# One-core layer kernel: query and key weights packed on chip, mask products in four row groups, padded one-hot and spreading matrices, new step orders

## The reference, cut to what matters

```
qm = split(q @ Wq.T + bq); km = split(k @ Wk.T + bk); vm = split(v @ Wv.T + bv)
scores = einsum(qm, km) / 4
scores = where(mask, scores, -1e8)
out = (softmax(scores) @ vm) @ Wo.T + bo
```

```
weights = one_hot(top1(logits)) * softmax(logits)
y = (gelu(x @ W_cols + b_cols) * weights).reshape(...) @ proj_w + proj_b + x
```

## Time and profile before

| what | value |
|---|---|
| median of three runs | 2304.79 us (2304.69 to 2305.6) |
| the profiled execution's own time | 2305.36 us |
| its span, first to last instruction | 2303.6 us |
| mean granted TensorE clock | 0.974 of full speed |
| PE, PEld, DVE, ACT, POOL busy | 92%, 78%, 72%, 60%, 34% |
| DMA | 30.12 MB, 33,954 packets, nearly all in the first 45 us |

### The profile page before, as it was taken

How to read it: one execution, slowest core, us unless ns; L and a number is a source line. 1 busy time by engine, 2 the same in 40 slices (tenths; PEclk the granted TensorE clock), 3 DMA queues, 4 the chain that set the end, 5 groups by cost and what they waited for, 6 DMA issues and landing times.

```text
span 2303.6 us, 81126 instructions
## 1 busy us (share of the span) xinstructions
PE 2130.6 (92%) x33068; PEld 1805.7 (78%) x33130; DVE 1657.9 (72%) x5290; ACT 1374.1 (60%) x4262; POOL 778.8 (34%) x1835
## 2 busy tenths in 40 slices
PE   4799999999999999999999999999999999999976
PEld 3687888888878777878888888878878878788864
DVE  3478777777777677777777877767877777777743
ACT  3465556766555765556776555666555666555642
POOL 2233243333233333233343324333324333224321
PEclk8799999999999999999999999999999999999997
DMA  6000000000000000000000000000000000000000
GB/s 208 7 8 10 10 10 7 5 9 10 10 10 7 4 9 10 10 10 7 5 9 9 10 10 7 4 9 10 10 10 7 4 9 9 9 10 7 7 4 5
DMA packets 33954, 30.12 MB, mean 13 GB/s; under 512 B 17680, under 2 KB 31008, under 8 KB 32816
## 3 DMA queue, kind: packets, MB, share of 16 engines
q1 hardware_dynamic: 33584, 24.94, 3.6%
...
## 4 chain that ended last, share of the span: by engine, by line
PE 77%; DVE 14%; ACT 4%; issue 3%; SPq 2%; POOL 1%; DVEq 0%; DMA 0%; POOLq 0%
PE bank_b L641 11%; PE bank_a L463 10%; PE bank_b L738 5%; PE bank_a L473 4%; PE bank_b L761 4%; PE bank_b L649 4%; PE bank_b L602 4%; DVE y1p L1142 3%; PE bank_a L579 3%; PE bank_a L535 3%; PE bank_a L511 3%; PE bank_b L692 3%; ACT prob L926 2%; PE bank_a L586 2%; PE bank_a L545 2%
## 5 line engine op out<-in xcount | busy, mean ns | idle before, releaser
L1013 DVE SCALAR_TENSOR_TENSOR acc<-ypad,convw,acc 128x128 f32<-128x128 f32 x1536 | 429.0, 343 | 112.4 <-ACT acc L815 112.1
L463 PE MATMUL bank_a<-xnT,wqkvz 128*128 128x128 f32 x2048 | 250.6, 279 | 2.0 <-DVE u L1089 2.0
L463 PEld LDWEIGHTS bank_a<-xnT,wqkvz 128*128 128x128 f32 x2048 | 241.4, 194 | 6.2 <-DVE u L1089 4.3
L926 ACT ACTIVATE prob<-bank_b,nmax 128x128 f32<-128x128 f32 x512 | 182.2, 381 | 39.4 <-DVE nmax L1163 38.6
L1378 POOL TENSOR_TENSOR ostat<-ostat 128x4 f32<-128x4 f32 x64 | 20.4, 320 | 504.3 <-ACT gseg L880 502.2
L1424 POOL TENSOR_SCALAR lnv<-mv 128x1 f32<-128x1 f32 x128 | 26.1, 204 | 362.5 <-DVE mv L1103 357.2
L815 ACT ACTIVATE acc<-bank_a,convw 128x128 f32<-128x128 f32 x512 | 148.0, 395 | 0.0
L535 PE MATMUL bank_a<-zblk,kkT 32*32 32x32 f32 x8192 | 119.5, 195 | 22.3 <-DVE zblk L1073 15.6
L906 ACT ACTIVATE prob<-bank_b 128x512 f32<-128x512 f32 x64 | 38.2, 597 | 167.4 <-PE bank_b L641 167.4
L535 PEld LDWEIGHTS bank_a<-zblk,kkT 32*32 32x32 f32 x8192 | 93.7, 107 | 55.8 <-issue 44.5
L545 PE MATMUL bank_a<-ablk,xblk 32*32 32x32 f32 x8192 | 120.0, 195 | 18.6 <-DMA bk<-in_bk_dram 15.1
...
## 6 DMA issues: line engine op xcount, KB each, us to landing
xin<-in_x_dram SPq DMA_DIRECT2D x32, 128.0 KB, 2.0
cin<-in_ctx_dram SPq DMA_DIRECT2D x32, 128.0 KB, 2.1
out_dram<-yout SPq DMA_DIRECT2D x32, 128.0 KB, 1.7
...
```

The lines of the kernel that those rows point to most:

```text
L463: last = mm(A[bank][:, b * P:(b + 1) * P], wqkvz[:, c, o:o + P], xnT[:, c, :], start=(c == 0), stop=(c == KC - 1))
L926: last = fn(prob[:, j, b, :], Bk[j][:, b * P:(b + 1) * P], ACT.Exp, scale=HD ** -0.5, bias=nmax[:, 4 * j + b:4 * j + b + 1], accum_out=esu ...
L1013: stt(acc[:, c, :], ypad[:, c, k:k + P], convw[:, c, k:k + 1], acc[:, c, :], ALU.mult, ALU.add).then_inc(conv.sem, 1)
```

## The change

1. `Wq` and `Wk` are loaded whole (512 KB each, zeros included) into the space of `probT` (named `raw`), two DMAs in place of 16; at the start of trip 2, after the wait for `w_b`, POOL copies the used columns in eight operations to `wq` and `wk`. `b_k` and `b_q` wait for it (`packed`) for the first element.
2. The mask product of bank `j` has 32 rows: a matrix whose rows 0, 32, 64 and 96 are one and whose others are zero (`row0_bf`) against rows 32j to 32j + 31 of `fill_bf`, in row group `j`.
3. `onehot` is 128 x 128 (columns 16 to 127 stay zero) and `wT` and `spread_bf` have 128 rows (rows 16 to 127 of `spread_bf` stay zero), so that the transpose, the copy and the spreading products use 128 rows and columns.
4. All four orders are new. The trips are cut at another point (greatest lag 2, so 34 trips), and steps have other neighbours.

```
+            ("iota", NCOL), ("parity", 2), ("row0", 1)):
+    put("row0", (p % 32 == 0) * 1.0)
 ORDER = dict(
-    pe="b_v@2 b_x2T@2 a_lb01@1 a_la10@1 b_router@2 b_gu0@2 b_gu1@2 a_la11@1 a_lb10@1 b_gu2@2 a_la20@1 "
-       "a_lb11@1 b_gu3@2 b_dn0@2 a_lb20@1 a_la21@1 b_dn1@2 a_lb21@1 a_vT0@1 a_la30@1 b_k@2 a_la31@1 a_lb30@1 "
-       "a_lb31@1 b_y1T@2 a_pa@1 b_q@2 a_pb@1 c_s a_mt@1 c_pT0 a_vT1@1 a_xT a_sz0@1 c_pT1 a_ba a_qkv0 c_pT2 "
-       "a_o0@1 a_sz1@1 c_pT3 a_qkv1 a_o1@1 c_pv c_R a_z0 a_z1 c_xo a_qkv2 a_qkv3 c_y2T a_dec0 c_h a_ss c_lg "
-       "c_c0 a_st c_c1 c_wT a_kk c_spread a_dec1 c_pj0 b_oT0 b_oT1 c_pj1 b_w0 b_w1 a_la00 b_cT a_qk a_la01 "
-       "a_lb00".split(),
-    act="b_sum@2 b_cT@2 b_x2T@2 b_sg0@2 b_rl@2 b_sg1@2 b_rt@2 a_mix2@1 a_mix3@1 a_sum b_y1T@2 a_zf@1 b_q@2 "
-       "a_zo@1 c_exp0 a_mt@1 c_exp1 a_xT c_exp2 a_sz0@1 c_exp3 a_ba a_qkv0 a_o0@1 a_sz1@1 c_pT0 c_pT1 a_qkv1 "
-       "a_o1@1 c_R a_ln a_z0 a_mix0 a_z1 a_seg a_mix1 a_sq c_y2T c_h a_qkv2 a_st c_lt a_qkv3 c_c0 c_te c_wT "
-       "c_c1 a_dec0 a_dec1 b_oT0 b_oT1".split(),
-    dve="a_lb31@1 a_pa@1 b_k@2 a_u0@1 c_y4@3 c_max0 c_max1 a_xn c_max2 a_low@1 a_u1@1 c_max3 c_pT0 a_conv00 "
-       "a_conv01 c_pT1 a_conv02 c_rec a_core0@1 a_conv10 c_ao a_conv11 a_core1@1 c_sum2 a_conv12 c_y2 c_lb "
-       "c_route a_conv20 a_ss c_gc0 c_weight c_gc1 a_lower a_init c_sum3 b_hid a_la00 c_y3 b_x2 a_la01 "
-       "a_lb00 a_conv21 b_v a_conv22 a_lb01 a_conv30 a_la10 a_conv31 a_la11 a_lb10 b_act0 b_top a_conv32 "
-       "a_la20 a_lb11 a_score b_act1 b_ys0 a_la21 a_lb20 b_ys1 a_lb21 a_la30 a_la31 b_y1 a_lb30".split(),
-    pool="c_y2b@3 a_rq@1 c_ln2@3 b_xh@2 b_rs@2 b_rd@2 b_rt@2 c_ln3@3 a_xr@1 b_ln0@2 b_y1b@2 a_x a_osc0@1 a_ga "
-       "a_osc1@1 a_g c_ln1 c_rx b_mask c_sig a_sc".split(),
+    pe="a_la11@1 b_gu3@2 a_lb11@1 a_la20@1 b_dn0@2 a_la21@1 a_lb20@1 b_dn1@2 a_lb21@1 a_la30@1 a_vT0@1 b_k@2 "
+       "a_la31@1 a_lb30@1 a_lb31@1 b_y1T@2 a_pa@1 b_q@2 a_pb@1 c_s a_mt@1 a_vT1@1 a_xT c_pT0 a_sz0@1 c_pT1 "
+       "a_ba a_qkv0 c_pT2 a_o0@1 a_sz1@1 c_pT3 a_qkv1 a_o1@1 c_pv c_R a_z0 a_z1 c_xo a_qkv2 a_qkv3 a_ss "
+       "c_y2T a_dec0 c_h a_st c_lg c_c0 c_c1 c_wT a_dec1 c_spread a_kk c_pj0 b_oT0 b_oT1 c_pj1 b_w0 b_w1 "
+       "a_la00 b_cT a_la01 a_lb00 b_v a_qk b_x2T a_lb01 a_la10 b_router b_gu0 b_gu1 b_gu2 a_lb10".split(),
+    act="b_sg1@2 b_rt@2 a_sum a_mix2@1 a_mix3@1 b_y1T@2 a_zf@1 b_q@2 a_zo@1 c_exp0 a_mt@1 c_exp1 a_xT c_exp2 "
+       "a_ba a_sz0@1 c_exp3 a_qkv0 a_o0@1 a_sz1@1 c_pT0 c_pT1 a_qkv1 a_o1@1 c_R a_ln a_mix0 a_z0 a_z1 a_mix1 "
+       "a_sq a_qkv2 a_st c_y2T c_h a_qkv3 c_lt a_seg c_c0 c_wT c_c1 c_te a_dec0 a_dec1 b_oT0 b_oT1 b_cT "
+       "b_sum b_x2T b_rl b_sg0".split(),
+    dve="a_lb10@1 b_act1@2 a_la20@1 a_lb11@1 b_ys0@2 a_la21@1 a_lb20@1 b_ys1@2 a_lb21@1 a_la30@1 a_la31@1 "
+       "b_y1@2 a_lb30@1 a_lb31@1 a_pa@1 b_k@2 a_u0@1 a_xn c_max0 c_max1 c_max2 a_low@1 a_u1@1 c_max3 c_pT0 "
+       "a_conv00 c_pT1 c_rec a_conv01 a_conv02 a_conv10 a_conv11 c_ao a_core0@1 a_core1@1 a_conv12 c_sum2 "
+       "c_y2 a_conv20 a_conv21 a_conv22 c_lb a_ss c_route c_gc0 c_weight c_gc1 a_lower a_init c_sum3 b_hid "
+       "a_la00 c_y3 b_x2 a_la01 a_lb00 a_conv30 a_conv31 b_v a_lb01 a_score a_la10 c_y4 b_top b_act0 "
+       "a_conv32 a_la11".split(),
+    pool="b_xh@2 a_rq@1 b_rd@2 a_xr@1 b_rt@2 b_ln0@2 a_x b_y1b@2 b_mask a_osc0@1 a_ga a_osc1@1 a_g c_ln1 c_y2b "
+       "c_rx c_sig a_sc c_ln2 b_rs c_ln3".split(),
 )
-        spread_bf = sb("spread_bf", [NCOL, 8 * P], BF16)
+        spread_bf = sb("spread_bf", [P, 8 * P], BF16)
+        row0_bf = sb("row0_bf", [P, P], BF16)
-        onehot = sb("onehot", [P, NCOL])
-        wT = sb("wT", [NCOL, P], BF16)
+        onehot = sb("onehot", [P, P])
+        wT = sb("wT", [P, P], BF16)
-        dense_qk = [(w[:, :, P * o:P * o + P].rearrange("p k (j c d) -> p k j c d", j=4, c=2)[:, i, :, c, :],
-                     w_d.rearrange("p k (a j t) -> p k a j t", a=4, j=4, t=32)[:, i, 2 * o + c, :, 0:HD])
-                    for w, w_d in ((wq, wq_d), (wk, wk_d)) for i in range(KC) for o in range(2) for c in range(2)]
+        raw = probT[:, :, :, :].rearrange("p a b f -> p (a b f)").rearrange("p (w k f) -> p w k f", w=2, k=KC)
+        raw_qk = [(raw[:, i, :, :], w_d) for i, w_d in enumerate((wq_d, wk_d))]
...
             def c_s(n):
-                    mm(quad(Bk[j]), ident_bf[:, :], fill_bf[:, :].unsqueeze(1).to_broadcast([P, 4, P]), start=True, stop=False)
+                    r = slice(32 * j, 32 * j + 32)
+                    mm(quad(Bk[j]), row0_bf[r, :], fill_bf[r, :].unsqueeze(1).to_broadcast([32, 4, P]), start=True, stop=False)
...
             def c_wT(n):
-                tr(Bk[0][0:NCOL, 0:P], onehot[:, :], ident).then_inc(wT_ps.sem, 1)
+                tr(Bk[0][:, 0:P], onehot[:, :], ident).then_inc(wT_ps.sem, 1)
...
-                fn(wT[:, :], Bk[0][0:NCOL, 0:P], ACT.Copy).then_inc(wT_ok.sem, 1)
+                fn(wT[:, :], Bk[0][:, 0:P], ACT.Copy).then_inc(wT_ok.sem, 1)
...
+            nc.vector.tensor_copy(row0_bf[:, :], con("row0").to_broadcast([P, P])).then_inc(prep.sem, 1)
+            nc.gpsimd.memset(spread_bf[:, :], 0.0).then_inc(filled.sem, 1)
+            nc.gpsimd.memset(onehot[:, :], 0.0).then_inc(filled.sem, 1)
...
             def before_b():
                 pool.wait_ge(w_b.sem, W_B)
+                for i, w in enumerate((wq, wk)):
+                    for o in range(2):
+                        for c in range(2):
+                            dense = w[:, :, P * o:P * o + P].rearrange("p k (j c d) -> p k j c d", j=4, c=2)[:, :, :, c, :]
+                            padded = raw[:, i, :, P * (2 * o + c):P * (2 * o + c) + P].rearrange("p k (j t) -> p k j t", j=4)[:, :, :, 0:HD]
+                            ts(dense, padded, 1.0, 0.0, ALU.mult, ALU.add).then_inc(packed.sem, 1)
```

More of the change, by code:

```diff
@@ L55 @@
                       ("level1", BLK), ("levels", len(LEVELS) * BLK), ("eye_blocks", BLK),
-                      ("iota", NCOL), ("parity", 2)):
+                      ("iota", NCOL), ("parity", 2), ("row0", 1)):
     CONST[_name] = (_at, _at + _width)
@@ L306, in build @@
         w_a, w_b = sig("weights_a"), sig("weights_b")
+        packed = sig("packed", 8)
         wqkvz_in = [sig(f"wqkvz_in{g}") for g in range(6)]
@@ L369, in build @@
         W_A = 16 * (len(loads_a) + len(small_a))
-        W_B = 16 * (len(loads_b) + len(small_b) + len(dense_wo) + len(dense_qk) + len(dense_b))
-        FILLS = 5
-        PREP = 7
+        W_B = 16 * (len(loads_b) + len(small_b) + len(dense_wo) + len(raw_qk) + len(dense_b))
+        FILLS = 7
+        PREP = 8
         def heads(t, half):
@@ L420, in _ @@
                 sp.dma_start(dst[:], src).then_inc(w_b.sem, 16)
-            for dst, src in small_b + dense_wo + dense_qk:
+            for dst, src in small_b + dense_wo + raw_qk:
                 sp.dma_start(dst, src).then_inc(w_b.sem, 16)
@@ L653, in b_k @@
                 pe.wait_ge(*ysum(n, 2))
+                if first(n):
+                    pe.wait_ge(*packed(1))
                 for b in range(2):
@@ L1210, in c_route @@
                 dve.wait_ge(*lchain(n, 4))
-                ts(onehot[:, :], con("iota"), lsm[:, 0:1], None, ALU.is_equal).then_inc(lchain.sem, 1)
+                ts(onehot[:, 0:NCOL], con("iota"), lsm[:, 0:1], None, ALU.is_equal).then_inc(lchain.sem, 1)
                 ts(lsm[:, 1:2], lmax[:, 0:1], -0.5, None, ALU.mult).then_inc(lchain.sem, 1)
@@ L1262, in _ @@
             nc.vector.tensor_copy(ident_bf[:, :], ident).then_inc(prep.sem, 1)
+            nc.vector.tensor_copy(row0_bf[:, :], con("row0").to_broadcast([P, P])).then_inc(prep.sem, 1)
             nc.vector.tensor_copy(quad(below_bf), con("below").unsqueeze(1).to_broadcast([P, 4, P])).then_inc(prep.sem, 1)
-            nc.vector.tensor_copy(spread_bf[:, :], spread_in).then_inc(prep.sem, 1)
+            nc.vector.tensor_copy(spread_bf[0:NCOL, :], spread_in).then_inc(prep.sem, 1)
             dve.wait_ge(ce_ps.sem, 1)
```

## The result

The changed kernel is slower: 2356.47 us median against 2305.19 for the kernel before in the same session, ratio 1.0217, 95% interval [1.0198, 1.0235].

A forecast was written before the change was run, and what follows sets the result against it. It took ACT's unbroken stretch to bound each trip, with PE beside it, and late weights the startup. Trips 9, start 11 and end 1 us gave 21 off 2305.4: 2284.4, median forecast 2284 us, range 2261 to 2297.

The forecast's parts named there:

- Mask products: PE's four mask products per trip: row groups overlap, so the slot of 0.97 us shrinks by 0.63.
- Where it goes next: PE behind the masks: `a_sz0` starts near 1035.35 instead of 1036.15, putting PE 0.8 us ahead and ACT 0.63.
- Weight loads: Startup: two weight DMAs replace sixteen, engines are released earlier, POOL packing costs 3.3 us; gain 11 us once.
- One-hot and spreading matrices: PE's padded one-hot transpose and spreading products: no time gained or lost.
- End: The last mask products, at the end of the run, take about a third of their time: 1 us gained.
- The trip's gain: Each of 31 trips gets 0.3 us shorter, 9 us in all.
- ACT's new order: ACT's reordered operations add waits, leaving 0.3 us per trip of the 0.63 by which the exponentials come earlier.
- ACT's wait before `c_wT`: Sign in ACT's queue: ACT, ready at about 1060.4, waits 0.6 us before the copy of `c_wT`.
- PE's wait before `c_lg`: Sign in PE's queue: PE waits about 0.4 us before `c_lg`, behind the gelu of `c_h`.
- DVE and POOL orders: Reordered DVE and POOL steps around taps and `core` stay hidden; `core1` ends near 1049.8, PE needs it at 1050.03.
- wait of 0.46 stays: PE's idle time before a merge level, between `x2` and the masks, stays at 0.46 us per trip.
- Slower: core behind the taps: Rival: DVE taps ahead of `a_core0` delay `a_qkv2`, each trip 0.67 us longer, 2314 us; chance 0.10.

The follow-up runs named there:

- e_pack: The kernel before with the packed weight loads alone; ratio 0.9972 to the kernel before.
- e_pad: The kernel before with the padding of the one-hot and spreading matrices alone; ratio 1.0001 to the kernel before.
- e_mask: The kernel before with the mask products in four row groups alone; ratio 0.9903 to the kernel before.
- e_levels: The changed kernel with a memset between DVE's taps, `b_v` ahead of `a_conv30`, and PE's merge levels in the old sequence; ratio 0.9869 to the kernel before.
- e_gap: The changed kernel with one small DVE memset between taps `a_conv02` and `a_conv10`, breaking the row of 16; ratio 0.9971 to the kernel before.
- e_parts: The changed kernel with the four old orders, keeping packed weights, row-group masks and padding; 2279 us, ratio 0.9869 to the kernel before.
- e_order: The kernel before with the four new orders alone, without the other parts; ratio 1.0154 to the kernel before.

## Why the prediction was wrong

**Right.** *Mask products*: 0.63 forecast, 0.74 measured for the slot (0.97 to 0.23). The 3.07x of the Trainium skill ("TensorE: Matmul & The Clock Gate", Measured speedup vs the span model) would have made it 0.29; the rows of the score products were the better guide. The fourth mask did wait for `qT`: it starts 0.16 us behind the first (1054.84), 0.05 after ACT's `qT` ends, where the other three start within 0.01. But the first score products did not wait for its end, as I had assumed, and so the slot stayed at 0.23. *Where it goes next*: `a_sz0` at 5.25 behind the masks for 5.30. *Weight loads*: 11 us forecast, 9.7 in the profile (8.3 for e_pack alone), packing 3.1 for 3.3. *One-hot and spreading matrices*: zero, and e_pad measures 1.0001; the load times of the Trainium skill (the same page, LDWEIGHTS (loading the stationary operand)) would have cost about 3 us if exposed, which that run (0.9989 to 1.0013) can hardly tell; in its trace the load takes 0.14 us for 0.09. *End*: 1 us forecast, 0.1 found, a small miss.

**Undersized.** The trip's gain, 0.3 us, because ACT's new order was to give half back. With ACT's old order the masks give 0.7 us a trip (e_mask), and with the new orders repaired, ACT's among them (e_levels), the whole stands where the parts in the old order stand: in trips at full clock 67.6 us against 67.5, where the kernel before has 68.2. So that term measured 0.6 to 0.7. Of its two signs, ACT's wait before `c_wT` came in the changed kernel (16.6 us in 32 times, 0.5 for 0.6), PE's wait before `c_lg` did not. ACT's order was not tried by itself.

**The step that failed** is "*DVE and POOL orders*": "Hidden, with 0.2 to spare". It counted DVE's operations and took POOL's at their durations in the old order. DVE came as counted: `a_core0` ends 18.4 us behind the masks of its trip (1073.10), so `a_core1` could have ended at 19.5, for 19.75 in my count, and PE wanted `a_qkv2` at 20.0 (1076.26 less its wait of 1.58), for 19.98. What was late was POOL's scale for `a_core1`, because the edit made a row of 16 taps that read two tensors each, and that row held up a POOL operation that reads SBUF, 2.74 us for 0.20. The cost as measured: 2.5% between the changed kernel and e_gap, 57 us, 1.9 for each of some 30 trips, of which 1.5 shows at full clock and some 0.2 is the clock. A second step that failed is in *ACT's new order*: PE's "wait of 0.46 stays". It rose (15.6 to 25.2 us over the run) with the levels' new sequence on PE, which I had not costed, and that sequence cost 11 to 17 us, most of it at the lower clock. My sum had no term for the clock at all. The wait for `vpad`, with `b_v` behind two tap steps in place of one, was missed too; its edit measured about 6 us, within the intervals.

**The rival that was right for a wrong reason.** "*Slower: core behind the taps*" named the place, the sign (PE waits before `a_qkv2` for `u`) and the direction, at 0.10 and 2314. Its mechanism, DVE's own queue, is ruled out: DVE sits idle 1.97 us in front of `a_core1`. So its price of 0.67 a trip was a third of the real one. Put together from the runs, the changed kernel is: parts -1.3%, the hold-up +2.5, `b_v` and the levels +1.0, together +2.2; measured +2.17. The agreement says no more than that e_levels and e_parts have the same ratio, since the hold-up, `b_v` and the levels were measured by taking them away one after the other. e_order stands by itself: it measures 1.0154 with an interval of 1.0109 to 1.0199, where `b_v` and the levels (+1.0%) and three hold-ups (+0.2%) would give 1.012. That is inside, if its other executions had as few, which no trace tells.

**The version that beats both** is e_parts: the three parts with the orders of before, 2279 us, 1.3% faster than the kernel before and 3.4% faster than the changed one. e_levels, the new orders with three small repairs, equals it.
